# Every second block of attention scores is added onto the scores that stand in its banks

## The reference, cut to what matters

```python
x = L0_attn_X                                        # (4, 1024, 128)
h = layernorm(x) * (1 + ca) + sa
qkv = h @ W_qkv + b_qkv                              # 16 heads, DK = 64
Q, K, V = split(qkv)
scores = einsum('bhqd,bhkd->bhqk', Q, K) / sqrt(64)  # 1024 x 1024 a head, 4 batches
out = einsum('bhqk,bhkv->bhqv', softmax(scores), V)
x = x + ga * (out @ W_fc + b_fc)
h = layernorm(x) * (1 + cb) + sb
x = x + gb * mixture_of_4_experts(h)                 # router, top 2 of 4
```

## Time and profile before

| | us |
|---|---|
| runs, median of 3 | 1739.32 (1736.06 to 1740.1) |
| the profiled execution, its time | 1737.47 |
| its span in the profile | 1735.8 |
| setup, until attention's first instructions | 43.7 |
| attention, until the router stage's first instructions | 43.7 to 1511.1 |
| router and experts | 1511.1 to 1735.8 |

### The profile page before, as it was taken

The page is one execution under the profiler, slowest core; times in us unless marked ns, Lnnn a source line. Parts: engine busy times, 40 slices in busy tenths (PEclk is TensorE's granted clock), DMA queues, the critical chain, the costliest instruction groups (busy, mean ns, idle before and its releaser), DMA issues. The chain is left out here.

```text
span 1735.8 us, 29414 instructions
## 1 busy us (share of the span) xinstructions
PE 1629.8 (94%) x9675; PEld 908.8 (52%) x9675; DVE 1245.4 (72%) x2049; ACT 854.2 (49%) x1176; POOL 1210.3 (70%) x583
## 2 busy tenths in 40 slices
PE   3799999999999999999999999999999999756996
PEld 2455555555555555555555555555555554344886
DVE  5577777777777777777777777777777777587887
ACT  4344444444454445445444544444445454326874
POOL 4377777778878777777777778778777777520134
PEclk8799999999999999999999999999999999868999
DMA  3100000000000000000000000000000001000101
GB/s 107 49 22 22 22 22 21 21 21 21 21 21 21 21 21 21 21 21 19 10 14 21 21 21 21 21 21 21 21 21 21 21 14 51 25 0 25 41 28 31
DMA packets 44498, 42.87 MB, mean 25 GB/s; under 512 B 11405, under 2 KB 38570, under 8 KB 44330
## 3 DMA queue, kind: packets, MB, share of 16 engines
q1 hardware_dynamic: 44304, 42.35, 7.2%
q10 hardware_dynamic: 154, 0.03, 0.0%
HBM read 11.95 MB, written 2.10 MB: 8 GB/s over the span
## 5 line engine op out<-in xcount | busy, mean ns | idle before, releaser
L529 POOL TENSOR_TENSOR ACC<-ACC,PR 128x1024 f32<-128x1024 f32 x382 | 909.8, 2382 | 177.0 <-ACT PR L575 159.6
L608 DVE TENSOR_REDUCE NMH<-ps_mx 128x2 f32<-128x1024 f32 x507 | 619.6, 1222 | 254.7 <-PE ps_mx L758 254.6
L575 ACT ACTIVATE PR<-ps_s 128x1024 f32<-128x1024 f32 x512 | 497.2, 1023 | 316.2 <-PE ps_s L778 315.6
L788 PE MATMUL ps_o<-PR,V 128*64 128x512 f32 x2048 | 509.0, 616 | 7.1 <-ACT PR L575 5.8
L788 PEld LDWEIGHTS ps_o<-PR,V 128*64 128x64 f32 x2048 | 105.4, 134 | 289.8 <-ACT PR L575 273.2
L529 POOL TENSOR_TENSOR ACC<-PR 128x1024 f32<-128x1024 f32 x64 | 150.8, 2356 | 142.5 <-ACT PR L575 142.5
L639 DVE RECIPROCAL SUM<-SUM 128x128 f32<-128x128 f32 x256 | 240.5, 941 | 7.3 <-ACT SUM L566 7.3
L758 PE MATMUL ps_mx<-KHI,QHI 64*128 64x512 f32 x1014 | 227.0, 443 | 2.2 <-DVE NMH L608 1.5
L772 PE MATMUL ps_s<-QHI,KHI 64*128 64x512 f32 x1024 | 203.0, 392 | 0.1
L774 PE MATMUL ps_s<-QLO,KHI 64*128 64x512 f32 x1024 | 201.8, 390 | 0.0
L776 PE MATMUL ps_s<-QHI,KLO 64*128 64x512 f32 x1024 | 201.4, 389 | 0.0
(11 more groups left out here) (194 smaller groups left out, 1767.8 us busy)
## 6 DMA issues: line engine op xcount, KB each, us to landing
hcur<-hT SPq DMA_DIRECT2D x32, 512.0 KB, 2.9
Wqk<-Wall_hi SPq DMA_DIRECT2D x32, 128.0 KB, 2.6
Wqk<-Wall_lo SPq DMA_DIRECT2D x32, 128.0 KB, 2.4
x<-in_L_attn_X SPq DMA_DIRECT2D x4, 512.0 KB, 5.3
Wv<-in_L_attn_W_qkv SPq DMA_DIRECT2D x32, 64.0 KB, 2.0
Wfc<-in_L_attn_W_fc SPq DMA_DIRECT2D x32, 64.0 KB, 1.8
hT<-in_L_attn_X SPq DMA_DIRECT2D x4, 512.0 KB, 6.0
out<-e_res SPq DMA_DIRECT2D x7, 256.0 KB, 2.3
```

What stands on the lines that cost most here:

```text
L529: G.tensor_tensor(ACC[:, ch, :, :], a, PR[:, t, :, :], ALU.add).then_inc(added, 1)
L575: A.activation(PR[:, t, :, :], ps_s[:, i:i + 2, :], ACT.Exp, scale=SCALE).then_inc(exp_done, 1)
L608: D.tensor_reduce(NMH[:, ch, i, kc, :], banks, AX, ALU.max, negate=True).then_inc(mx_red, 1)
L788: last = T.matmul(ps_o[half(h), ch, :], V[:, u, t, half(h)], PR[:, t, h, :], start=(t == 0), stop=(t == 7))
```

## The change

Let t be a key tile whose number modulo 4 is 2 or 3. Its scores go to the same two banks as those of tile t-2, which ACT has read by then but which still stand there, maximum subtracted. Before, they were computed afresh. Now PE adds (K of tile t minus K of tile t-2)·Q onto them. The part ONE·QN isn't needed there, so these steps have six matmuls in place of eight. They are the steps of the odd blocks.

The difference of keys comes from a projection of its own: in the setup, `dT` = hT of columns 256 to 511 less those of 0 to 255, in each group of 512 (a bias cancels), split into `dT_hi` and `dT_lo`; in the attention stage a new unit "d" of 256 columns for each chunk (three matmuls; ACT writes DHI, DVE writes DLO). KLO is now only needed for the tiles computed afresh, so its step on DVE has 256 columns in place of 512. Since a bank has to keep its scores from an even block to the next odd one, nothing else may write to it in between: the sums move from blocks 0 and 4 to the ends of blocks 1 and 5, and `INVERT` and `NORMALISE` move with them. The units are placed anew: k now borrows bank 1, d bank 2, v stands where fc stood and fc where v did. In `first`, two d units are made too. In the setup, ACT and POOL split `Wall` early instead of last, and the split of `dT` comes last. To make room, Q has three buffers of 512 in place of two of 1024, and NMW one in place of two.

```diff
+            halves = g.hT[:, :].rearrange("p (c k) -> p c k", k=512)
+            for b in range(B):
+                cc = slice(2 * b, 2 * b + 2)
+                dve.wait_ge(s_h, 2 * b + 2)
+                V.tensor_tensor(dT[:, cc, :], halves[:, cc, 256:512], halves[:, cc, 0:256], ALU.subtract).then_inc(s_d, 1)
...
+            act.wait_ge(s_wall, 16)
+            for ty in range(2):
+                A.activation(g.Wall_hi[:, :, ty, :, :], Wall[:, :, :, ty, :], ACT.Copy).then_inc(s_whi, 1)
             act.wait_ge(s_const, 2)
             act.wait_ge(s_mv, 1)
             A.activation(sd[:, :], mv[:, :, 1], ACT.Sqrt, bias=g.eps[:, 0:1]).then_inc(s_sd, 1)
...
+            for b in range(B):
+                cc = slice(2 * b, 2 * b + 2)
+                act.wait_ge(s_d, b + 1)
+                A.activation(g.dT_hi[:, cc, :], dT[:, cc, :], ACT.Copy).then_inc(s_dhi, 1)
...
-            run_pairs(pool, GROUPS, body)
             pool.wait_ge(s_whi, 2)
...
+            run_pairs(pool, GROUPS, body)
+            for b in range(B):
+                cc = slice(2 * b, 2 * b + 2)
+                pool.wait_ge(s_dhi, b + 1)
+                nc.gpsimd.tensor_tensor(g.dT_lo[:, cc, :], dT[:, cc, :], g.dT_hi[:, cc, :].bitcast(F32), ALU.subtract)
...
-        UNITS = {0: (("k", 1, 0, 2), ("rows", 0, 0, 0), ("fc", -1, 0, 3)),
-                 2: (("k", 1, 1, 2), ("v", 1, 0, 3)),
-                 4: (("q", 1, 0, 2), ("rows", 0, 1, 0), ("fc", -1, 1, 3)),
-                 6: (("q", 1, 1, 2), ("v", 1, 1, 3))}
-        SUMS = {0: (-1, 1), 4: (0, 0)}
+        UNITS = {0: (("k", 1, 0, 1), ("d", 1, 0, 2), ("rows", 0, 0, 0), ("v", 1, 0, 3)),
+                 2: (("k", 1, 1, 1), ("d", 1, 1, 2), ("fc", -1, 0, 3)),
+                 4: (("q", 1, 0, 2), ("rows", 0, 1, 0), ("v", 1, 1, 3)),
+                 6: (("q", 1, 1, 2), ("fc", -1, 1, 3))}
+        SUMS = {1: (-1, 1), 5: (0, 0)}
...
-        NORMALISE = {3: (-1, 1), 7: (0, 0)}
+        NORMALISE = {4: (-1, 1), 0: (-1, 0)}
...
-                        if t == 2 and has(n - 1):
+                        if t == 5 and has(n - 1):
...
+                elif kind == "k":
+                    dve.wait_ge(k_hi, 2 * m + ch + 1)
+                    D.scalar_tensor_tensor(KLO[:, u, ch, :], ps_w[:, 0:256], bias[:, u, 1:2],
+                                           KHI[:, u, ch * 512:ch * 512 + 256].bitcast(F32),
+                                           op0=ALU.add, op1=ALU.subtract).then_inc(k_lo, 1)
+                elif kind == "d":
+                    dve.wait_ge(d_hi, 2 * m + ch + 1)
+                    D.tensor_tensor(DLO[:, u, ch, :], ps_w[:, 0:256], DHI[:, u, ch, :].bitcast(F32), ALU.subtract).then_inc(d_lo, 1)
...
+                normalise(NP - 1, 0)
                 unit("fc", NP - 1, 1, 0, ps_s[:, 0, :])
...
+                elif kind == "d":
+                    T.matmul(ps_w[:, 0:256], wh, hi, start=True, stop=False)
+                    T.matmul(ps_w[:, 0:256], wl, hi, start=False, stop=False)
+                    T.matmul(ps_w[:, 0:256], wh, lo, start=False, stop=True).then_inc(d_proj, 1)
...
-                for h in range(2):
-                    last = T.matmul(ps_s[:, i + h, :], ONE[half(h), :], QN[half(h), ch, :], start=False, stop=True)
+                if whole:
+                    for h in range(2):
+                        last = T.matmul(ps_s[:, i + h, :], ONE[half(h), :], QN[half(h), ch, :], start=False, stop=True,
+                                        skip_group_check=True)
```

More of the change, by code:

```diff
@@ L361, in sem @@
             return ctx.enter_context(nc.semaphore(name))
-        QHI = sb("QHI", [P, 2, L], F32R)
-        QLO = sb("QLO", [P, 2, L], F32R)
+        QHI = sb("QHI", [P, 3, 512], F32R)
+        QLO = sb("QLO", [P, 3, 512], F32R)
         KHI = sb("KHI", [P, 2, L], F32R)
-        KLO = sb("KLO", [P, 2, L], F32R)
+        KLO = sb("KLO", [P, 2, 2, 256], F32R)
+        DHI = sb("DHI", [P, 2, 2, 256], F32R)
+        DLO = sb("DLO", [P, 2, 2, 256], F32R)
         QN = sb("QN", [P, 2, 512], F32R)
@@ L657, in pair @@
                 for b in range(8):
-                    for kind, m, v, ch, bank in reversed(units_of(n, u, b)):
-                        if kind != "fc":
+                    for kind, m, v, ch, bank in units_of(n, u, b):
+                        if kind == "rows":
+                            unit(kind, m, v, ch, ps_s[:, bank, :])
+                    for kind, m, v, ch, bank in units_of(n, u, b):
+                        if kind in ("k", "d", "q"):
                             unit(kind, m, v, ch, ps_s[:, bank, :])
@@ L755, in max_both_heads @@
                 wait(pe, mx_red, count - ahead)
-                q = ch * 512 + i * P
                 for h in range(2):
-                    last = T.matmul(banks[:, h, :], QHI[half(h), u, q:q + P], KHI[half(h), u, kc * 512:(kc + 1) * 512],
+                    last = T.matmul(banks[:, h, :], QHI[half(h), buf(u, ch), i * P:i * P + P], KHI[half(h), u, kc * 512:(kc + 1) * 512],
                                     start=True, stop=True)
@@ L769, in scores @@
                         pe.wait_ge(k_lo, 2 * n + 2)
[L770 removed]
+                        pe.wait_ge(d_lo, 2 * n + 2)
+                i = 2 * k
+                whole = t % 4 < 2
+                if whole:
+                    hi, lo = KHI[:, u, t * P:(t + 1) * P], KLO[:, u, c, k * P:(k + 1) * P]
+                else:
+                    hi, lo = DHI[:, u, c, k * P:(k + 1) * P], DLO[:, u, c, k * P:(k + 1) * P]
                 for h in range(2):
[L772 removed]
+                    T.matmul(ps_s[:, i + h, :], hi[half(h)], QHI[half(h), buf(u, ch), :], start=whole, stop=False, skip_group_check=True)
                 for h in range(2):
[L774 removed]
+                    T.matmul(ps_s[:, i + h, :], hi[half(h)], QLO[half(h), buf(u, ch), :], start=False, stop=False, skip_group_check=True)
                 for h in range(2):
[L776 to L778 removed]
+                    last = T.matmul(ps_s[:, i + h, :], lo[half(h)], QHI[half(h), buf(u, ch), :], start=False, stop=not whole,
+                                    skip_group_check=True)
+                if whole:
+                    for h in range(2):
+                        last = T.matmul(ps_s[:, i + h, :], ONE[half(h), :], QN[half(h), ch, :], start=False, stop=True,
+                                        skip_group_check=True)
                 last.then_inc(scored, 1)
@@ L807, in pair @@
                     for kind, m, v, ch, bank in units:
+                        if bank == SUMS_BANK and b - 1 in SUMS and has(n + SUMS[b - 1][0]):
+                            pe.wait_ge(sums_in, 2 * (n + SUMS[b - 1][0]) + SUMS[b - 1][1] + 1)
                         unit(kind, m, v, ch, ps_s[:, bank, :])
```

81 lines of the change are left out of this document (44 added, 37 removed).

## The result

The changed kernel takes 1745.5 us (median of 8 runs, 1742.4 to 1751.1), the kernel before on the same chip 1735.7 (8 runs, 1732.5 to 1740.1). The ratio is 1.0054, with a 95% interval of 1.0036 to 1.0072: slower by 9.4 us (6.2 to 12.5). The time that was said, 1743, lay in a frame in which the kernel before took 1739.3, and meant 3.7 us more, by the sum 4.8. That 1743 is only 2.5 off is in part luck, since its frame was 3.6 us high.

A forecast was written before the change was run, and what follows sets the result against it. Odd blocks were taken as a chain of maxima and first scores, first exponent, then `times_v`. Terms of -29.4 + 23.1 + 6.2 + 2.0 + 1.4 + 1.5 gave +4.8 us, 1742.3, said as 1743; range 1731 to 1762.

The forecast's parts named there:

- the sum 4.8: All priced terms together, -29.4 + 23.1 + 6.2 + 2.0 + 1.4 + 1.5 us, on the profiled execution's 1737.5.
- Odd blocks, -29.4: Odd attention blocks go from 4.47 to 4.24 us; only the group ahead of the first exponent is gained, 29.4 us.
- d units, +23.1: Two uncovered d units a pair on PE, 0.37 us each at 0.124 a matmul, 62 units: 23.1 us more.
- 1764: Rival: a d matmul on PE costs what one of 512 columns costs, 20.5 us more, 1764; chance 0.10.
- KLO in block 0, +6.2: PE's first scores in block 0 wait for DVE's KLO: 0.2 us a pair, 6.2 in all.
- DVE's queue behind KLO: Block 0: DLO, reduction and normalising step end at 5.05 us against the exponent's 5.0; a tie, taken at nothing.
- The rival on DVE: DVE's queue ahead of `times_v` becomes block 0's bound: 0.5 us a pair, 15.5 more, 1758; chance 0.13.
- Setup, +2.0: Setup: normalised rows start 0.9 us later beside Wall_lo, and dT steps on POOL and DVE add 1.1.
- First units, +1.4: Two d units in `first`, at the low clock: six matmuls of 0.23 us, 1.4 more.
- The last pair and the end, +1.5: At the end, chunk 0's normalising (0.69 us) and fc's matmuls come ahead of the last sums: 1.5 more.
- fc and v change places: Block 4 of attention: fc (about 1.0 us) and v (0.99) swap places on PE; no cost was counted.
- The sums come at the end of odd blocks instead of even ones, with the same matmuls: Attention loop: the moved sums wait for POOL's adds, which have a block more; no cost was counted.

The follow-up runs named there:

- the two experiments with one group less: Kernel before, without the KHI·QLO score group in odd blocks: left out of the first step, 1708.8 us; left out of the second step, 1735.3 us.
- rows first: The change with the transposed-maxima unit (rows) ahead of k and d in block 0 on PE: 1743.8 us, ratio 1.0031 to the kernel before.
- the experiment without d: The change without d units and dT; DVE takes the key differences from k's own projection: 1721.8 us, ratio 0.9916 to the kernel before.
- the last two kernels: Key differences from k's projection, gate steps and last normalising moved early: 1719.6 us when run again; the same with sums in bank 1, not 3: 1703.0 us.

## Why the prediction was right, and where it was short

**Odd blocks, -29.4: right.** 4.24 to 4.26 against 4.24 said; the first group counts, the second doesn't, as the two experiments with one group less show. `times_v` waits for the exponent as told, 0.51 behind the maxima where 0.60 was said; the 0.10 stand ahead of the maxima. In the last pair, the counterpart of the earlier trace rows, PE's idle time grew from 0.28 to 0.51 us:

```profile
1503.02 0.50 PE L824 MATMUL ps_s<-QHI,DHI 64*128 64x512 f32 x2
...
1505.18 1.99 PE L843 MATMUL ps_o<-PR,V 128*64 128x512 f32 x8 [0.51 <-ACT PR L602]
```

**d units, +23.1: right.** 0.36 and 0.35 a unit in the timeline, 0.345 by doubling them. The price of v's passes was the right row to go by. The rule that a weight load overlaps only with another row group (the Trainium skill, TensorE: Matmul & The Clock Gate, "The mechanism") would have given 1764; d's loads use all rows and its matmuls start 0.12 apart, so taken as it stands it doesn't hold here. The same section also lets a load for the background weight buffer go ahead; no run here tells whether that is what happens.

**KLO in block 0, +6.2: the right wait, its size about two thirds.** In the timeline 0.03 ahead of the scores and 0.10 in the distance to the next group, 0.13 (0.2 was said), some 4 us in all; with rows first the pair gained 0.20, of which 0.14 are KLO's. Against it the pair's sum -0.84 (odd blocks, four times 0.21) + 0.71 + 0.13 = 0, and measured is -0.02.

**DVE's queue behind KLO: no wait, as taken.** O ends at 615.75, 4.62 into the block where 5.05 was said, 0.26 ahead of the exponent's end at 616.01, so it isn't quite a tie. KLO takes 0.47 and DLO 0.41, and the five steps from QN to O take 3.15 us together while their durations add up to 3.48: each starts before the one ahead of it is over by the profile, and the prediction added durations. `times_v` there starts at 616.24 with 0.17 of wait for the exponent, as it had in block 0 before: 0.17 there too. The rival on DVE fell with these sizes.

**Setup, +2.0, measured +2.45.** The right mechanism, some 0.45 small. The weights are there in time, and the normalised rows collide with Wall_lo as told (2.70 for the eight that took 2.14). By the sixth of the eight pieces of `hT` the delay has grown to 1.75 us (ACT begins it at 33.97 instead of 32.22; 0.9 was said). POOL's work behind it is 0.7 longer than before (1.1 was said): its last three steps of hT_lo, beside DVE's dT, take 5.38 where one takes 1.27 alone, and dT_lo takes 4.92 where Wall_lo took 4.64. DVE's steps of four columns take 1.2 us each beside it, the answer to the row of 1.25 in the earlier trace rows, and DVE is done at 45.90, POOL at 45.87: which of the two ends the setup is not shown.

```profile
35.61 5.38 POOL L194 TENSOR_TENSOR hT_lo<-hT,hT_hi  x3 [2.93 <-ACT hT_hi L241]
40.95 4.92 POOL L204 TENSOR_TENSOR dT_lo<-dT,dT_hi 128x512 fp32r<-128x512 f32 x4
```

```profile
19.97 2.70 DVE L301 TENSOR_SCALAR xn<-x,mv,rs 128x128 f32<-128x128 f32 x8
...
41.05 1.20 DVE L317 TENSOR_SCALAR tmpT<-tmpT 128x4 f32<-128x4 f32 x1
```

**First units, +1.4, measured +0.55.** The low clock of the earlier trace rows ended in the middle of d: its matmuls start 0.21, 0.16 and then 0.12 apart. d takes 0.84 us in all, and v behind it, now at the full clock throughout, takes 0.28 less than before. When the clock rises isn't the change's doing: in the second profile of the change it was at 1.00 before d began, in the middle of k and q.

```profile
54.27 0.41 PE L766 MATMUL ps_mx<-dT_hi,Wqk 128*128 128x256 f32 x1
54.48 0.33 PE L767 MATMUL ps_mx<-dT_hi,Wqk 128*128 128x256 f32 x1
54.64 0.28 PE L768 MATMUL ps_mx<-dT_lo,Wqk 128*128 128x256 f32 x1
```

**The last pair and the end, +1.5, measured +2.3 behind the last joined maxima and +1.1 ahead of them.** fc and O behind the adds are as told: from the last `times_v` to the last sums 6.17 instead of 5.04 us, 1.1 more. What wasn't seen is that "fc and v change places", taken at nothing, isn't free in the last pair, where there is no k, d, q or v left. fc, first in its block, waits 0.70 for ACT's read of the sums, in blocks 2 and 6, which is the same wait that the experiment without d found in every pair. The first scores wait for QN, 0.40 in block 0 and 0.83 in block 4, where fc covered it before. In the second profile of the change the clock fell from 1.00 to 0.50 during this fc (0.74 in the mean from 1509.4 to 1511.0, 0.50 behind that), and the stretch behind the last joined maxima cost 3.5 more than before instead of 2.3.

```profile
1487.60 0.50 PE L824 MATMUL ps_s<-QHI,KHI 64*128 64x512 f32 x2 [0.83 <-DVE QN L660]
...
1497.64 1.12 PE L783 MATMUL ps_s<-O,Wfc 128*128 128x512 f32 x2 [0.70 <-ACT SUM L593]
...
1510.30 1.13 PE L783 MATMUL ps_s<-O,Wfc 128*128 128x512 f32 x2 [3.12 <-DVE O L679]
```

**Missed: pair 1, +3.4.** This is the step that failed. "The sums come at the end of odd blocks instead of even ones, with the same matmuls" priced the move of the sums at nothing and asked only what they wait for. They were also cover: 0.96 us of PE work between the second maxima of an even block and the first of the odd one, in which DVE could be late. In the other pairs nothing needs it; in pair 1 a gate step of 2.8 us does, twice. The third wait, 1.09 on QN, came from DVE's order: `INVERT` moved a quarter of the inversion ahead of a gate step, and this step ran longer beside POOL's add. The gate steps weren't in the prediction at all. With them out of the way the pair lost 3.7 us of its length; that experiment doesn't part the two causes, which rest on the distances in the trace.

So the 9.24 us are the sum's 4.8, and 3.4 (pair 1) + 0.45 (setup) + 1.1 (last pair, ahead of the last joined maxima) + 0.8 (behind them) - 0.85 (first units) - 0.4 (pairs 2 to 29, -0.54 measured where -0.1 was said of all pairs): together 4.4 more. The last two are luck as far as the sum is concerned. What stays open is a few us of the medians: the gate steps' 4.5 us show in the trace and not in the median, and the last two kernels differ by 16.6 us in the median and 10.1 in the attention loop.

## What to carry to other kernels

Ask of each group of PE work whether it stands ahead of or behind the point at which the next engine starts: the same 0.23 us was worth 28 us in one place and nothing in the other. Price work that you move also as cover, for what was hidden under it in the rare iterations as in the common ones: look for the one iteration that carries extra work. And what it costs to add a piece of work (d twice: 0.69 a pair) isn't what its removal brings (block 2 without d: 0.07 of 0.35), since a wait may stand right behind it; the bank that the next unit borrows was worth about as much as the unit (0.33 a pair). The last iteration, in which work runs out, deserves the same look: four waits of 0.4 to 0.8 us stood there where other work had covered them.

## What the runs showed of the hardware

A matmul of 256 columns with a weight load of 128 x 128 starts 0.115 to 0.12 us apart from the next at the full clock, half of the 0.235 of 512 columns: the load is hidden at this size too, since doubling these matmuls cost 0.115 each. A DVE step with two inputs in SBUF stands still for the whole of a POOL add that began first: 2.80 us against 0.69 for the same step alone. PE's granted clock is 0.50 (1.2 GHz) over the first units' k and q matmuls (49 to 54 us) and 1.00 (2.4 GHz) from 55 to 60, and in a second profile of the same kernel already 1.00 from 53, so an addition to these units is cheaper at their end than at their start, and its price varies from execution to execution. So does that of fc and the sums behind an idle stretch of 3.1 us of PE at the end of attention: fc took 1.05 us at a clock of 1.00 in one profile of the change, 1.31 in the other, where the clock fell to 0.50 meanwhile, and 2.01 at 0.50 in the first run with the differences from the keys. And the untouched last stages vary by 8 us between profiled executions, more than most of the terms here, so that a change in the stages ahead of them is better read where attention ends than at the end of the span.
